# Second layer's attention as straight-line code, in batches of six key tiles instead of four

## The chip, the core and the metric

The kernel runs on one core of a Trainium2 chip. The metric is the device time of the whole program in microseconds (us), the median of several runs. TensorE (PE in the profile) multiplies matrices into PSUM, VectorE (DVE), ScalarE (ACT) and GpSimd (POOL) do elementwise work, SyncE (SP) issues most of the DMAs. Each engine works through its own list of instructions in order, and the lists are tied together by semaphores that the kernel sets by hand.

## The reference

Two layers, each with attention and a feed-forward network (FFN) that gates it, on x of shape (2, 2048, 256), 16 heads of width 16. What the change touches is the attention of the second layer:

```python
Q = _l2norm(heads(Wq)); K = _l2norm(heads(Wk)); V = heads(Wv)
cos_sim = jnp.clip(jnp.einsum('bhtd,bhsd->bhts', Q, K), -0.999, 0.999)
scores = 1.0 - jnp.arccos(cos_sim) / jnp.pi
W = jnp.power(jnp.maximum(scores, EPS), 16.0)
W = W / (jnp.sum(W, axis=-1, keepdims=True) + EPS)
out = jnp.einsum('bhts,bhsd->bhtd', W, V)          # then @ Wo.T + bo
...
x = x + s * silu(ffn(xn))                          # s: attention, xn: layernorm(x)
```

So for each of 2 x 16 pairs of batch entry and head there is a 2048 x 2048 matrix of cosines, and each element goes through a clip, an arccosine and a sixteenth power. The first layer has another weight function (inverse squared distances), which is the same before and after.

## The kernel before, in words

**Phases.** `program` runs one phase after another, each a block with a barrier at its end: constants, then for each layer `weights_phase`, `norm_phase`, `projection_phase`, `attention_phase`, `output_phase`.

**Units.** In the attention a *unit* is one key tile of 128 keys against all 2048 queries of one head and one batch entry: a [128, 2048] float32 matrix. A head has 32 units (16 for each batch entry), the layer 512. Sixteen units make one *tile of work* n (a head and a batch entry); with each n goes one 128-token tile of the FFN. There are 32 of them.

**Steps of a unit in the second layer.** TensorE writes the cosines into two PSUM halves `psS[0]`, `psS[1]` of 1024 columns (`pe_scores`, L741). VectorE clips each half into the ring in SBUF (L1049) and multiplies clipped by unclipped cosine into a ring of squares (L1058); only then may TensorE overwrite that half. ScalarE takes `Ln(1 - c^2)` (L1006) and a `Sigmoid` of it (L1011). VectorE multiplies (L1089, here called the tangents). ScalarE takes `Arctan` (L1016). The power of 16 is split by columns: ScalarE does columns 0 to 1311 by `Ln` (L1022) and `Exp` (L1028), VectorE 1312 to 1535 by an affine step (L1069) and four squarings (L1073), GpSimd 1536 to 2047 the same way (L711, L715). TensorE then multiplies with the values (`pe_values`, L764), into `psO`.

**Batches.** `Ln`/`Exp` and `Sigmoid`/`Arctan` belong to different tables of ScalarE, so the steps are done for a *batch* of 4 units at a time, and a table is loaded twice in a batch (`ACT_TABLE_LOAD` ahead of L1011 and at L1017). ScalarE's order in a batch is two `Ln`, load, four `Sigmoid`, two `Arctan`, load, two `Ln`, two `Exp`. VectorE's order is: clip and square batch j, powers of batch j-1, tangents of batch j. So in each batch the tangents wait for the sigmoids (`s_rs`), and the second `Ln` waits for the last squares (`s_q`). The ring has 8 slots of cosines and 4 of squares.

**Heads.** `pairs` writes head 0 and head 15 out and runs heads 1 to 14 in a hardware loop on SP, TensorE, ScalarE and VectorE; GpSimd's heads are written out. A loop's code for a head begins with another load of ScalarE's table (L1001).

**The FFN's part.** `pe_hidden` (L785, L791: 16 matmuls and two bias matmuls) comes on TensorE behind a batch's scores and the previous batch's weighted sums, in batches 2 and 6 of a head; `pe_ffn_sum` (L800, L803) a batch later. ScalarE's `act_relu` (L817), `act_out` (L810) and `act_ffn_out` (L823, L825) come between batches; VectorE's `dve_out` comes behind the tangents.

**Buffers.** `values` and `gated` (each [128, 32, 256]) are buffers of their own, `work` holds three times that size. The values of the second layer stay in `values`, GpSimd copies a head's part into `v_tile` (L703). The normalized head outputs go into `gated`, from which `output_phase` transposes them (L1154).

## Time and profile before

| what | us |
|---|---|
| median of 3 runs | 7601.04 (7600.39 to 7608.52) |
| the profiled execution: its own time | 7607.89 |
| the profiled execution: span of the trace | 7605.8 |
| first clip of the second layer's attention (L1049) starts at | 3018.2 |
| last clip of it starts at | 7474.3 |
| VectorE busy over the whole span | 7175.8 (94%) |
| ScalarE busy | 6931.5 (91%) |
| TensorE busy, matmuls | 4245.9 (56%) |
| GpSimd busy | 2209.8 (29%) |

The span runs from the first to the last instruction; the 2 us between it and the own time lie outside the trace. The second layer's attention takes well over half of the time. Shares of busy time are averages: which engine sets the pace of a batch has to be read from the timelines.

### The profile page before, as it was taken

The numbers are of one execution on the slowest core, as the hardware profiler recorded it, in microseconds if no ns is written. First come the engines' busy times: TensorE is split into PE (matmuls) and PEld (weight loads), VectorE is DVE, ScalarE is ACT, GpSimd is POOL, SyncE is SP. The second block draws the span as 40 slices with busy tenths as digits, with TensorE's granted clock in tenths as the row PEclk, the third lists the DMA queues.
The fourth block names the chain that finished last, engine by engine and source line by source line (L and its number), as shares of the span: only waits on it lengthen the run. The fifth ranks groups of instructions, "written<-read, shape, count | busy, mean of one in ns | idle before, by whom it ended". The sixth has DMA issues, their size and how long they took to land. (4 is left out here: it accounts for less than half of the span.)

```text
span 7605.8 us, 60658 instructions
## 1 busy us (share of the span) xinstructions
PE 4245.9 (56%) x17232; PEld 1292.8 (17%) x17232; DVE 7175.8 (94%) x6927; ACT 6931.5 (91%) x4385; POOL 2209.8 (29%) x1348
## 2 busy tenths in 40 slices
PE   6666666676766667444444454444444444544545
PEld 3221212121222233111111111111111111111112
DVE  7899999999999966999999999999999999999996
ACT  3799999999999934999999999999999999999995
POOL 0000000000000000454544445454544545454452
PEclk9888888888888878666566665656666665665667
DMA  3100000000000022000000000000000000000002
GB/s 128 43 18 11 16 12 16 12 16 12 16 12 14 10 102 102 6 11 7 6 11 6 6 11 6 6 11 6 6 11 6 10 6 6 10 6 6 10 2 69
DMA packets 113675, 148.41 MB, mean 20 GB/s; under 512 B 17038, under 2 KB 98857, under 8 KB 112634
## 3 DMA queue, kind: packets, MB, share of 16 engines
q1 hardware_dynamic: 104314, 138.54, 5.8%
q10 hardware_dynamic: 9216, 8.39, 0.3%
q14 instruction: 109, 0.89, 0.0%
q8 instruction: 36, 0.59, 0.0%
HBM read 91.55 MB, written 55.31 MB: 19 GB/s over the span
## 5 line engine op out<-in xcount | busy, mean ns | idle before, releaser
L741 PE MATMUL psS<-q_stack,k_stack 102*128 102x512 bf16 (+1 forms) x4096 | 1795.1, 534 | 2464.6 <-DVE work L1058 1617.3
L715 POOL TENSOR_TENSOR work<-work 128x1024 f32<-128x1024 f32 x1024 | 1915.4, 1907 | 10.2
L764 PE MATMUL psO<-work,v_tile 128*32 128x512 f32 x8192 | 1432.5, 822 | 732.0 <-DVE work L1073 727.5
L933 DVE SCALAR_TENSOR_TENSOR work<-work,psS 128x1024 f32<-128x1024 f32 x1024 | 1240.2, 1211 | 42.4 <-ACT work L891 41.9
L1049 DVE TENSOR_SCALAR work<-psS 128x1024 f32<-128x1024 f32 x1024 | 1206.7, 1218 | 71.0 <-issue 41.2
L1058 DVE TENSOR_TENSOR work<-psS,work 128x1024 f32<-128x1024 f32 x1024 | 1199.8, 1213 | 0.0
L1089 DVE SCALAR_TENSOR_TENSOR work<-work 128x2048 f32<-128x2048 f32 x512 | 1138.5, 2285 | 58.3 <-ACT work L1011 56.7
L891 ACT ACTIVATE work<-psS 128x1024 f32<-128x1024 f32 x1024 | 1099.6, 1074 | 70.6 <-PE psS L741 45.4
L1006 ACT ACTIVATE work<-work 128x4096 f32<-128x4096 f32 x256 | 921.2, 3612 | 126.9 <-DVE work L1058 117.1
L906 ACT ACTIVATE work<-work 128x2048 f32<-128x2048 f32 x512 | 1005.3, 1964 | 0.4 <-ACT ffn_out L823 0.4
L741 PEld LDWEIGHTS psS<-q_stack,k_stack 102*128 102x128 bf16 (+1 forms) x4096 | 257.5, 105 | 4136.7 <-DVE work L1058 2509.8
L1011 ACT ACTIVATE work<-work 128x2048 f32<-128x2048 f32 x512 | 936.0, 1899 | 1.4
L711 POOL TENSOR_SCALAR work<-work 128x1024 f32<-128x1024 f32 x256 | 267.5, 1045 | 2300.4 <-ACT work L1016 2290.2
L1016 ACT ACTIVATE work<-work 128x4096 f32<-128x4096 f32 x256 | 924.0, 3609 | 6.9
L703 POOL COPY v_tile<-values 128x256 f32<-128x256 f32 x64 | 28.4, 444 | 2996.5 <-PE psO L764 2313.0
L952 DVE TENSOR_TENSOR work<-work 128x1056 f32<-128x1056 f32 x512 | 639.2, 1249 | 0.0
L946 DVE TENSOR_SCALAR work<-work 128x2048 f32<-128x2048 f32 x512 | 623.1, 1217 | 0.0
L1022 ACT ACTIVATE work<-work 128x2624 f32<-128x2624 f32 x256 | 597.9, 2383 | 1.4
L1028 ACT ACTIVATE work<-work 128x2624 f32<-128x2624 f32 x256 | 595.7, 2374 | 0.0
L1073 DVE TENSOR_TENSOR work<-work 128x448 f32<-128x448 f32 x1024 | 571.8, 624 | 0.0
L913 ACT ACTIVATE work<-work 128x992 f32<-128x992 f32 x512 | 558.0, 1090 | 0.0
L764 PEld LDWEIGHTS psO<-work,v_tile 128*32 128x32 f32 x8192 | 253.0, 137 | 1579.4 <-issue 856.5
(126 smaller groups left out, 3444.8 us busy)
## 6 DMA issues: line engine op xcount, KB each, us to landing
qk_parts<-work SPq DMA_DIRECT2D x64, 384.0 KB, 3.2
q_stack<-qk_parts SPq DMA_DIRECT2D x384, 64.0 KB, 2.2
k_stack<-qk_parts SPq DMA_DIRECT2D x384, 64.0 KB, 2.2
ffn_in<-xT_store SPq DMA_DIRECT2D x64, 128.0 KB, 2.5
y_store<-ffn_out ACTq DMA_DIRECT2D x64, 128.0 KB, 1.7
work<-y_store SPq DMA_DIRECT2D x8, 1024.0 KB, 12.0
work<-in_x SPq DMA_DIRECT2D x1, 4096.0 KB, 14.4
xn_store<-work SPq DMA_DIRECT2D x1, 4096.0 KB, 13.0
```

Of the source, the lines that this page charges most:

```text
L715: nc.gpsimd.tensor_tensor(part, part, part, ALU.mult).then_inc(s_pp, 1)
L741: last = nc.tensor.matmul(m.psS[half][:, q * 512:(q + 1) * 512], m.k_stack[b][0:rows, kt * P:(kt + 1) * P], m.q_stack[b][0:rows, c:c + 512 ...
L764: last = nc.tensor.matmul(m.psO[b][VW * q:VW * (q + 1), :], m.v_tile[b][:, kt, :], ring[:, u % RING, q * 512:(q + 1) * 512], start=kt == 0 ...
L891: nc.scalar.activation(ring[:, u % RING, half * 1024:(half + 1) * 1024], m.psS[half][:, :], ACT.Abs_reciprocal_sqrt, bias=ZERO_SHIFT)\
L906: nc.scalar.activation(slot, slot, ACT.Abs_reciprocal_sqrt, bias=SHEP_EPS * SHEP_EPS, scale=2 * SHEP_EPS).then_inc(s_v, 1)
L933: nc.vector.scalar_tensor_tensor(part, part, 0.5 / SHEP_EPS, m.psS[half][:, :], ALU.add, ALU.mult).then_inc(s_y, 1)
L1006: nc.scalar.activation(pair, pair, ACT.Ln, bias=1.0, scale=-1.0).then_inc(s_ls, 1)
L1011: nc.scalar.activation(slot, slot, ACT.Sigmoid, scale=-0.5).then_inc(s_rs, 1)
L1016: nc.scalar.activation(pair, pair, ACT.Arctan).then_inc(s_at, 1)
L1049: nc.vector.tensor_scalar(ring[:, u % RING, half * 1024:(half + 1) * 1024], m.psS[half][:, :], COS_MAX, -COS_MAX, ALU.min, ALU.max)\
L1058: nc.vector.tensor_tensor(q_ring[:, u % BATCH, cols], m.psS[half][:, :], ring[:, u % RING, cols], ALU.mult).then_inc(s_q, 1)
L1089: nc.vector.scalar_tensor_tensor(slot, q_ring[:, u % BATCH, :], RSIN_MAX, slot, ALU.min, ALU.mult).then_inc(s_z, 1)
```

## The change

What it does:

1. `attention_phase` becomes two functions. `distance_phase` is the first layer's, as it was. `cosine_phase` is new and holds the second layer's; its code is written out for all 512 units on all engines (no hardware loop).
2. Batches have 6 units (`sizes` is 4, then 84 times 6, then 4: 86 batches instead of 128). The ring has 18 slots: 2 x 6 of cosines, 6 of squares. Batches no longer end where a tile of work ends.
3. ScalarE's instructions get larger: `Ln` and `Arctan` take half a batch (3 units, 6144 columns), `Sigmoid` two units, the power's `Ln` and `Exp` 3 x 1312 columns. The table of `Ln`/`Exp` is named again at the start of each batch. VectorE's and GpSimd's parts of the power take 3 x 224 and 3 x 512 columns. GpSimd's first step waits for the first half of the arctangents only.
4. VectorE's order in pass i is: tangents i, head output, clip and square i+1, powers i. That is the order of before, with the pass cut elsewhere.
5. TensorE: `ffn_hidden` stands in the middle of a batch's scores. Weighted sums, head output and `ffn_sum` stand behind them.
6. To make room, `values` and `gated` become parts of `work`. In the second layer the values go to DRAM (`v_store`) during the projection, and a head's part is loaded into `v_tile` by SP in pieces of 64 bytes. Each head output is stored to DRAM (`o_store`) from a small stage by a DMA that ScalarE issues, and `output_phase` loads it back, as a third load in each of its four chunks. There the transposes wait for that load.

```diff
+        self.work = sb("work", [P, 5 * NT * D])
+        self.values = self.area(3 * NT * D, NT, D)
+        self.gated = self.area(4 * NT * D, NT, D)
...
@@ projection_phase, SP
+                if L == 1:
+                    sp.wait_ge(s_vfree, 4 * i + 6)
+                    sp.dma_start(io["v_store"][:, bass.ds(4 * i, 4), :], m.values[:, bass.ds(4 * i, 4), :])\
+                        .then_inc(s_vst, 16)
...
@@ cosine_phase
+    BATCH = 6
+    LANES = 18
+    sizes = [4] + [BATCH] * ((TOTAL - 8) // BATCH) + [4]
+    starts = [sum(sizes[:j]) for j in range(len(sizes) + 1)]
+    last_batch = {n: batch_of(KT * n + KT - 1)[0] for n in range(TILES)}
+    last_batch[-1] = -2
...
+        def _(sp):
+            for n in range(TILES):
+                h, b = n // B, n % B
+                if n >= B:
+                    sp.wait_ge(s_qk, 2 * KT * (n - 1))
...
+                if n >= B:
+                    sp.wait_ge(s_pv, KT * (n - 1))
+                sp.dma_start(m.v_tile[b][:, :, 0:DH], v_view[:, b, :, h, :]).then_inc(s_vt[b], 16)
+                if n > 0:
+                    sp.wait_ge(s_h, 2 * n)
+                sp.dma_start(m.ffn_in[:, :, :], io["xT_store"][:, :, n * P:(n + 1) * P]).then_inc(s_fin, 16)
...
+        def _(pe):
+            scores(0)
+            for i in range(NB + 2):
+                ahead = range(starts[i] + 1, min(starts[i + 1] + 1, TOTAL)) if i < NB else []
+                middle = len(ahead) // 2
+                for g in ahead[:middle]:
+                    scores(g)
+                for n in range(TILES):
+                    if last_batch[n - 1] + 3 == i:
+                        ffn_hidden(n)
+                for g in ahead[middle:]:
+                    scores(g)
+                if 1 <= i <= NB:
+                    for g in range(starts[i - 1], starts[i]):
+                        weighted(g)
+                for n in range(TILES):
+                    if last_batch[n] + 2 == i:
+                        head_out(n)
+                    if last_batch[n - 1] + 3 == i:
+                        ffn_sum(n)
...
+        def _(act):
+            for i in range(NB + 2):
+                if i < NB:
+                    nc.scalar.preload_act_table_set("natural_log_exp_and_others")
+                    for c, (p, size) in enumerate(thirds(i)):
+                        act.wait_ge(s_q, 2 * (starts[i] + p + size))
+                        nc.scalar.activation(square(p, size), square(p, size), ACT.Ln, bias=1.0, scale=-1.0)\
+                            .then_inc(s_ls, 1)
+                    for p, size in couples(i):
+                        act.wait_ge(s_ls, 2 * i + (1 if p + size <= sizes[i] // 2 else 2))
+                        nc.scalar.activation(square(p, size), square(p, size), ACT.Sigmoid, scale=-0.5)\
+                            .then_inc(s_rs, 2)
+                    for p, size in thirds(i):
+                        act.wait_ge(s_z, starts[i] + p + size)
+                        nc.scalar.activation(cosine(i, p, size), cosine(i, p, size), ACT.Arctan).then_inc(s_at, 1)
+                    nc.scalar.preload_act_table_set("natural_log_exp_and_others")
...
+                for n in range(TILES):
+                    if last_batch[n - 1] + 2 == i:
+                        relu(n)
+                    if last_batch[n] + 1 == i:
+                        out_copy(n)
+                    if last_batch[n] + 2 == i:
+                        out_store(n)
+                    if last_batch[n - 1] + 3 == i:
+                        ffn_out(n)
...
+        def _(dve):
+            for g in range(starts[1]):
+                clip_and_square(g)
+            for i in range(NB + 2):
+                if i < NB:
+                    tangents(i)
+                for n in range(TILES):
+                    if last_batch[n] + 2 == i:
+                        head_out(n)
+                if i + 1 < NB:
+                    for g in range(starts[i + 1], starts[i + 2]):
+                        clip_and_square(g)
+                if i < NB:
+                    powers(i)
...
@@ output_phase
-        n_loads = 3 if L == 0 else 2
+        n_loads = 3
...
+                else:
+                    sp.dma_start(m.gated[:, t, :], io["o_store"][:, t, :]).then_inc(s_load[c], 16)
...
+                if L == 1 and n % CP == 0:
+                    pe.wait_ge(s_load[n // CP], 16 * n_loads)
```

(`thirds` gives a batch's two halves, `couples` its pairs of units.)

TensorE's order around the FFN's hidden layer, before: the end of head 15's first half. L741 are scores (16 matmuls are 4 units), L764 weighted sums, L785 and L791 the hidden layer, L800 and L803 the FFN's sum.

```order
L764 MATMUL psO<-work,v_tile 32x512 x16
L741 MATMUL psS<-q_stack,k_stack 128x512 x16
L764 MATMUL psO<-work,v_tile 32x512 x16
L785 MATMUL psM<-ffn_in,w1T 128x128 x8
L791 MATMUL psM<-ident,b_tiles 128x512
L785 MATMUL psM<-ffn_in,w1T 128x128 x8
L791 MATMUL psM<-ident,b_tiles 128x512
L741 MATMUL psS<-q_stack,k_stack 128x512 x16
L764 MATMUL psO<-work,v_tile 32x512 x16
```

The same place of the program after: L1005 are scores (24 matmuls are 6 units), L1023 weighted sums, L1044 and L1046 the hidden layer.

```order
L1031 MATMUL psM<-ident,head_outT 128x128 x4
L1005 MATMUL psS<-q_stack,k_stack 128x512 x12
L1044 MATMUL psM<-ffn_in,w1T 128x128 x8
L1046 MATMUL psM<-ident,b_tiles 128x512
L1044 MATMUL psM<-ffn_in,w1T 128x128 x8
L1046 MATMUL psM<-ident,b_tiles 128x512
L1005 MATMUL psS<-q_stack,k_stack 128x512 x12
L1023 MATMUL psO<-work,v_tile 32x512 x24
L1053 MATMUL psM<-w2T,hidden 128x256 x8
```

Before, the hidden layer stood between weighted sums and the next batch's scores. Now it stands between the third and the fourth of six units of scores.

ScalarE's order in one batch, before (L1006 `Ln`, L1011 `Sigmoid`, L1016 `Arctan`, L1022 and L1028 the power):

```order
L1006 ACTIVATE work<-work 128x4096 x2
L1011 ACT_TABLE_LOAD
L1011 ACTIVATE work<-work 128x2048 x4
L1016 ACTIVATE work<-work 128x4096 x2
L1017 ACT_TABLE_LOAD
L1022 ACTIVATE work<-work 128x2x1312 x2
L1028 ACTIVATE work<-work 128x2x1312 x2
```

and after (L1112, L1116, L1120, L1125 and L1129 in their place):

```order
L1109 ACT_TABLE_LOAD
L1112 ACTIVATE work<-work 128x6144 x2
L1116 ACT_TABLE_LOAD
L1116 ACTIVATE work<-work 128x4096 x3
L1120 ACTIVATE work<-work 128x6144 x2
L1121 ACT_TABLE_LOAD
L1125 ACTIVATE work<-work 128x3x1312 x2
L1129 ACTIVATE work<-work 128x3x1312 x2
```

Eleven instructions now serve six units where twelve served four; there are three table loads in each batch instead of two (and one more in each head).

## Rows read from the trace of the kernel before

**Rows 1.** Busy time by engine in a stretch of the cosine attention.

```profile
5000.00:7400.00 2400.00, 1134.05 (x4290) 294.20 (x4286) 2334.68 (x2105) 2328.97 (x1038) 1172.40 (x702) 0.61 0.03 7
```

**Rows 2.** Where line L1049 waited, second layer's clips, DVE; first and last start.

```profile
L1049 DVE TENSOR_SCALAR work<-psS x1024: 1210/1216/1226, 3018.2 to 7474.3; 128x1024 f32<-128x1024 f32 x171
...
  issue: 41.2, 13
```

**Rows 3.** ScalarE's timeline: start us, length us, engine, line, operation, count, idle before.

```profile
4009.70 7.12 ACT L1006 ACTIVATE work<-work 128x4096 f32<-128x4096 f32 x2 [0.62 <-ACT ffn_out L823]
...
4047.61 3.62 ACT L1006 ACTIVATE work<-work 128x4096 f32<-128x4096 f32 x1 [0.46 <-DVE work L1058]
...
4051.24 1.28 ACT L1011 ACT_TABLE_LOAD   x1
...
4052.54 7.31 ACT L1011 ACTIVATE work<-work 128x2048 f32<-128x2048 f32 x4
...
4059.75 7.27 ACT L1016 ACTIVATE work<-work 128x4096 f32<-128x4096 f32 x2
...
4068.34 4.67 ACT L1022 ACTIVATE work<-work 128x2624 f32<-128x2624 f32 x2
```

**Rows 4.** ScalarE's sigmoid of one unit, from the page's groups: mean ns.

```profile
L1011 ACT ACTIVATE work<-work 128x2048 f32<-128x2048 f32 x512 | 936.0, 1899 | 1.4
```

**Rows 5.** VectorE's timeline over the same batches.

```profile
4047.49 2.71 DVE L1069 TENSOR_SCALAR work<-work 128x448 f32<-128x448 f32 x2
...
4050.12 4.36 DVE L1073 TENSOR_TENSOR work<-work 128x448 f32<-128x448 f32 x8
...
4054.48 8.90 DVE L1089 SCALAR_TENSOR_TENSOR work<-work 128x2048 f32<-128x2048 f32 x4
...
4064.45 2.34 DVE L1049 TENSOR_SCALAR work<-psS 128x1024 f32<-128x1024 f32 x2
...
4082.82 1.96 DVE L1069 TENSOR_SCALAR work<-work 128x448 f32<-128x448 f32 x2
```

**Rows 6.** GpSimd's timeline: its chain of squarings in that batch.

```profile
4034.95 15.00 POOL L715 TENSOR_TENSOR work<-work 128x1024 f32<-128x1024 f32 x8
```

**Rows 7.** VectorE's squarings of the last batch, while GpSimd runs its own.

```profile
7499.66 17.93 DVE L1073 TENSOR_TENSOR work<-work 128x448 f32<-128x448 f32 x8
```

**Rows 8.** TensorE's timeline around one hidden layer of the feed-forward part.

```profile
4089.11 5.46 PE L764 MATMUL psO<-work,v_tile 128*32 128x512 f32 x32 [5.12 <-DVE work L1073]
...
4094.50 2.05 PE L785 MATMUL psM<-ffn_in,w1T 128*128 128x128 f32 x16
...
4099.52 1.12 PE L791 MATMUL psM<-ident,b_tiles 8*128 8x512 f32 x2
...
4102.39 0.60 PE L741 MATMUL psS<-q_stack,k_stack 96*128 96x512 bf16 x2 [1.74 <-DVE work L1058]
...
4107.00 2.16 PE L741 MATMUL psS<-q_stack,k_stack 96*128 96x512 bf16 x4 [2.45 <-DVE work L1058]
```

**Rows 9.** Windows: TensorE's granted clock (PEclk) after 4089.11, when weighted sums began.

```profile
4088.00:4092.00 4.00, 2.89 (x16) 0.79 (x20) 3.25 (x3) 4.00 (x3) 0.00 (x0) 0.50 0.00 0
...
4092.00:4096.00 4.00, 4.00 (x33) 1.94 (x26) 4.00 (x3) 4.00 (x3) 0.00 (x0) 0.90 0.00 0
```

**Rows 10.** TensorE, output phase: the same eight matmuls at either clock.

```profile
7542.95 3.78 PE L1171 MATMUL psO<-hidden,w1T 128*128 128x256 f32 x8 [7.31 <-ACT w1T L1187]
...
7548.40 1.99 PE L1171 MATMUL psO<-hidden,w1T 128*128 128x256 f32 x8
```

**Rows 11.** Output phases of first and second layer: first DMA issue, last ScalarE copy.

```profile
2713.72 0.39 SPq L1128 DMA_DIRECT2D hidden<-in_woT  x1
...
2789.55 0.60 ACT L1187 ACTIVATE w1T<-psS 128x512 f32<-128x512 f32 x1 [2.81 <-PE psO L1171]
...
7529.76 0.39 SPq L1128 DMA_DIRECT2D hidden<-in_woT  x1
...
7594.85 0.60 ACT L1187 ACTIVATE w1T<-psS 128x512 f32<-128x512 f32 x1 [2.81 <-PE psO L1171]
```

More of the change, by code:

```diff
@@ L60, in __init__ @@
         self.w2T = sb("w2T", [P, FT, D])
-        self.values = sb("values", [P, NT, D])
-        self.gated = sb("gated", [P, NT, D])
-        self.work = sb("work", [P, 3 * NT * D])
+        self.work = sb("work", [P, 5 * NT * D])
+        self.values = self.area(3 * NT * D, NT, D)
+        self.gated = self.area(4 * NT * D, NT, D)
         self.q_stack = [sb(f"q_stack{b}", [P, T], BF16) for b in range(B)]
@@ L643, in attention_phase @@
     LAG_INV, LAG_SQ = 2, 3
-    ACT_POW, DVE_POW = 1312, 1536
-    POW_STEPS = 10
-    BATCH = 4
     ACT_SQ = 992
-    rows = ROWS + NORM_ROWS if L == 0 else ROWS
-    loads = 2 * len(PRODUCTS) + (2 if L == 0 else 0)
+    rows = ROWS + NORM_ROWS
+    loads = 2 * len(PRODUCTS) + 2
     values = m.values[:, :, :].rearrange("p (b k) (h d) -> p b k h d", b=B, h=HEADS)
     gated = m.gated[:, :, :].rearrange("p (b q a) (h d) -> p b q a h d", b=B, q=QB, h=HEADS)
-    EPS_SUM = SHEP_EPS if L == 0 else SUM_EPS1
     with ExitStack() as ctx:
@@ L699, in _ @@
         def _(pool):
[L700 to L729 removed]
+            def head(h, first, last):
+                for b in range(B):
+                    if not first:
+                        pool.wait_ge(s_pv, UNITS * h + KT * b + KT - UNITS)
+                    nc.gpsimd.tensor_copy(m.v_tile[b][:, :, 0:DH], values[:, b, :, h, :]).then_inc(s_vt, 1)
+            pairs(pool, head)
         def pe_scores(pe, h, u, first, halves=(0, 1)):
@@ L736, in pe_scores @@
                 if not (first and u == 0):
-                    pe.wait_ge(s_y if L == 0 else s_q, 2 * (UNITS * h + u) + half - 1)
+                    pe.wait_ge(s_y, 2 * (UNITS * h + u) + half - 1)
                 for q in range(2):
@@ new lines, in dve_out, with head @@
+            nc.vector.tensor_tensor(out, ps[:, :, :, 0:DH], out, ALU.mult).then_inc(s_g0, 1)
+            dve.wait_ge(s_g0, n + 1)
+            nc.vector.tensor_tensor(out, out, rec16, ALU.mult).then_inc(s_g, 1)
+        OUT_COPY, OUT_T, OUT_DIV = 5, 7, 8
+        HID = (0, 1, 2, 3)
+        RELU, SQ = (2, 4), (4, 6)
+        SUM = {8: (0,), 9: (1,), 10: (2,), 11: (3,), 12: (4,), 13: (5,), 14: (6, 7)}
+        COPY = 15
+        @block.tensor
+        def _(pe):
+            def head(h, first, last):
+                for u in range(UNITS + (LAG_PV if last else 0)):
+                    b, kt = u // KT, u % KT
+                    n = 2 * h + b
+                    if u < UNITS:
+                        pe_scores(pe, h, u, first, (0,))
+                    if not (first and u < LAG_PV):
+                        pe_values(pe, h, u - LAG_PV, first)
+                    if u < UNITS:
+                        pe_scores(pe, h, u, first, (1,))
+                    if kt == 0 and not first:
+                        pe.wait_ge(s_g, n - 1)
+                    if kt == 2 and not (first and b == 0):
+                        pe.wait_ge(s_yo, n)
+                    if kt in HID and u < UNITS:
+                        pe_hidden(pe, n, (HID.index(kt),))
+                    if kt == OUT_T and u < UNITS and not (first and b == 0):
+                        pe.wait_ge(s_r, 2 * n + 1)
+                        pe_out(pe, n - 1)
+                    if kt in SUM:
+                        pe_ffn_sum(pe, n, SUM[kt])
+                if last:
+                    pe_out(pe, 2 * HEADS - 1)
+            pairs(pe, head)
```

577 lines of the change are left out of this document (284 added, 293 removed).

## The prediction, made before the run

> **What bounds the kernel now.** I read the windows first, then the clips' own line, then the engines' timelines over two batches. In a stretch of 2400 us VectorE is busy 2334.68 and ScalarE 2328.97, TensorE 1134.05, GpSimd 1172.40 [rows 1]. Two engines at 97% means that shares alone cannot say which one sets the pace. The clips give it: from 3018.2 to 7474.3 lie 127 batches, three units and one half [rows 2]. A unit of clips and squares takes (4082.82 - 4064.45) / 4 = 4.59 us [rows 5], so the last 3.25 units are 14.95, and a batch takes (4456.1 - 14.95) / 127 = 34.97 us, 8.74 per unit.
>
> Why 34.97? There are two sums. *VectorE's own work*: clips 18.37, powers 6.99 (4047.49 to 4054.48), tangents 8.90 and 0.10 behind them [rows 5]: 34.4. *The chain through both engines*: last square, 0.12 until the second `Ln` starts (4047.61), 3.62 of `Ln`, 1.30 from load to sigmoid (4051.24 to 4052.54) [rows 3], 1.90 for one sigmoid [rows 4], 0.04, tangents and gap 9.00, clips 18.37 [rows 5]: 34.4 as well. The two are level: the powers fill the 7.0 us in which ScalarE does `Ln`, load and first sigmoid. On top come a head output every fourth batch (1.07 us from the tangents' end to the next clip, 0.97 more than the gap; 0.24 per batch) and 41.2 us in 13 waits on "issue", which are the loop's restarts (0.32 per batch) [rows 2, 5]. Sum 34.96, measured 34.97.
>
> **The change part by part.**
>
> *Size of instructions.* ScalarE's cost grows by (3.62 - 1.90) / 2048 = 0.84 ns per column [rows 3, 4]. So an `Ln` of 6144 columns takes 5.34, a sigmoid of two units 3.62, a power step of 3936 columns 3.48 (2.38 for 2624). ScalarE has less to do per unit. But what VectorE must wait for is longer: the half batch of `Ln` behind the last square and the first sigmoid both grow.
>
> *The chain for six units*: 0.12 + 5.34 + 1.30 + 3.62 + 0.04 + tangents 13.35 + 0.10 + clips 27.56 = 51.43 us, 8.57 per unit against 8.60. The larger batch halves nothing: the fixed part went from 7.0 for four units to 10.4 for six. VectorE's own sum: 27.56 + 13.45 + powers. Eight squarings of 448 columns took 4.36 [rows 5], 0.545 each; 224 more columns at 1.09 ns (8.90 / 8192) make 0.79, so 6.3. The two affine steps took 2.71 because GpSimd's chain was still running (4034.95 + 15.00 = 4049.95) [rows 5, 6]; with GpSimd at 1.5 times the work it ends about as late behind the clips, so 2.7 again. Powers 9.0, VectorE 50.0. The chain is longer by 1.4, so the chain sets the pace and VectorE idles 1.4 per batch.
>
> *ScalarE's own path*, from the first sigmoid (time 0): sigmoids until 10.7, `Arctan` of the first half until 16.0; the second half needs all tangents (3.66 + 13.35 = 17.0) and ends at 22.4; load 23.7; four power steps 13.7: 37.4; the repeated load 38.7; first `Ln` 44.0. The last square comes at 44.7. So the third load fits, with 0.8 to spare. What stands between batches (the copies and their DMAs) can exceed this: `ffn_out` costs 0.62 of idle time around its DMA and its copy, about 1.0 together [rows 3], and meets a head copy of the same kind in a third of the tiles: some 8 us in all.
>
> The skill puts a table switch higher: the Trainium skill, "ScalarE: Activation LUTs", section "What ACT_TABLE_LOAD costs", gives about 1.28 us for the load and 1.38 for a drain, 2.66 in all. By that each batch's chain would be 1.4 longer (+115 us) and ScalarE's path, with three of them, 4 longer. The rows show 1.30 from load to next instruction, and the sum goes by them.
>
> *Sum over the batches.* 83 steps from six to six: 4268.7. The step from four to six has two tangents less (4.45): 47.0. The step from six to four has two clips less and a smaller `Ln` (9.18 + 1.72): 40.5. Together 4356. The first clips and `Ln` are the same four units as before (23.4). Head outputs 31 x 0.97 = 30. So 4410 from first clip to last sigmoid, against 127 x 34.97 + 23.4 = 4464.6 before: -55. About 41 of this is the loop's waits.
>
> *The hidden layer in the middle of the scores.* In the steady state TensorE scores a unit in 2.16 us and then idles 2.45 until VectorE frees the next half [rows 8]. VectorE starts on that half as soon as it is written, so 2.45 us, and about 0.5 more, is all the cover there is. The hidden layer runs from 4094.50 to 4099.52 + 1.12 = 6.14 us [rows 8]. Before, it lay beside powers and tangents: scores then still waited 1.74 for VectorE [rows 8]. Now it lies between two units that VectorE clips one after the other. And 6.14 is at the high clock, since weighted sums from 4089.11 on had raised it: the granted clock was 0.50 in the first window and 0.90 in the second, so it rose at about 4092.8, 3.7 us after they began [rows 8, 9]. Scores alone run at the low clock. Eight matmuls take 3.78 at the low and 1.99 at the high level, a factor of 1.90 [rows 10]. If the hidden layer does 4.0 us at the low level, it gets 2.1 us of work done there and takes 8.0 in all. It is late by 8.0 - 2.45 = 5.55; the next scores, now at the high clock, are 0.44 faster (0.60 against 1.04), and ends overlap a little: VectorE stalls 5.0 us. Bounds: high clock throughout 6.14 - 2.45 - 0.44 = 3.2; low clock throughout 11.7 - 2.45 = 9.2. The stall delays the clips, which are in the chain, and 32 tiles have it: +160 us (102 to 294). It is the largest term. ScalarE's relu waits for it but still reaches the `Ln` in time.
>
> The clock rule of the Trainium skill, "TensorE: Matmul & The Clock Gate", section "The HAM clock gate", is that a busy array gets 2.4 GHz and one that pauses falls to 1.2. Taken alone it does not say which level the hidden layer would meet behind scores that come with pauses; the windows show the low one, and the sum goes by them.
>
> *Values and outputs through DRAM.* The values' load is asked for when the tile before last is weighted, a whole tile (about 137 us) ahead: hidden. SP's waits for it hold back the next stacks by some units at most, of 16. The value stores in the projection are hidden but for the last (+2). At the end ScalarE's last store has to land before the barrier: +4. The output phase gets a third load in each chunk. The first layer has that form: from first DMA to last copy 75.8 us against 65.1 [rows 11]: +10.7, and 1.5 for transposes that now wait. Together +18. If this were all hidden it would be 0.
>
> **Sum.** -55 + 160 + 8 + 18 = +131 on the profiled execution's 7607.9: 7739. The median of before lies 6.9 lower, so 7732; I say 7730.
>
> **Rivals.**
>
> *A, the hidden layer is slower or faster than thought, loop as above.* Its bounds give 7730 - 58 = 7672 and 7730 + 134 = 7864. A low clock to the end needs the rise to come later than the 3.7 us seen.
>
> *B, ScalarE's path decides* (reserve 0.8 us). If the repeated load or the issue of the head's store, 2048 pieces of 64 bytes, takes 1 us more in every batch, the loop grows by 0.2 x 84 = 17; if a store holds ScalarE for 3 us, by up to 60: 7750 to 7790. Against it: the store falls into the time in which the relu waits for the hidden layer anyway.
>
> *C, GpSimd and VectorE get in each other's way.* GpSimd now starts with the first half of the arctangents, at 16.0, while VectorE's last tangent runs until 17.0. In the last batch VectorE's eight squarings took 17.93 instead of 4.36 while GpSimd ran [rows 5, 7]. If GpSimd got in ahead of that tangent, each batch would lose its affine step of about 1.6: +134, 7865. The last tangent begins 1.3 us earlier than GpSimd asks, so I expect GpSimd to be the one that waits. The Trainium skill, "SBUF — State Buffer", section "SBUF: two separate sides", calls the port pair that the two share an exclusive lock that whoever starts first holds to its end, also against a VectorE instruction with two SBUF inputs. By that rule too the tangent wins here, as long as the order stands.
>
> *D, the other side: no stall.* If scores written ahead covered the hidden layer, only -55 + 8 + 18 = -29 would be left: 7572. It decides below 0.9 us of stall per tile. Speaking for it: before, no clip waits for it. Against: there are only two halves of PSUM, and each is asked for within 4.62 us.
>
> **How the numbers follow.** Forecast (stall 4 to 6, loop by the chain) 0.50, around 7730 +- 35. A low 0.17, A high 0.13, B 0.08, C 0.05, D 0.05, a shorter chain that ends level 0.02. Range for 8 in 10: 7660 to 7830; it takes in A's low end and most of its high one, B, and leaves out C and D. A measurement of this kernel can tell about 0.2% from no change. Faster by over 0.2% comes from D and some of the last: 0.06; within 0.2% 0.04; slower 0.90.
>
> **What the profile after would show.** Clips' pitch per unit in plain batches 8.57, with ScalarE's second `Ln` waiting about 0.8 us for the square, and VectorE's tangents waiting about 1.4 for the sigmoid. In each tile one clip idle for 5 us behind TensorE's scores, in sum 160. The hidden layer's matmuls at 8 us, half of it at clock 0.5. No "issue" waits at heads. Three table loads in a batch, 1.28 each. An output phase of 76 to 78 us. Wrong would be: a clip's wait of 3 or 9 (clock), tangents that overlap GpSimd's first step (C), squares that wait for nothing (B).

## The result and the profile after

| | us |
|---|---|
| median before, 4 runs on the same chip | 7600.89 (7600.39 to 7608.52) |
| median after, 4 runs | 7718.45 (7715.76 to 7728.88) |
| ratio | 1.0155, 95% interval 1.0137 to 1.0172 |
| profiled execution after: own time, span | 7728.88, 7727.1 |

The changed kernel is slower by 118 us, 1.55%; the forecast was 7730. The profiled execution is the longest of the four.

The page of the profile after: busy times, the places where VectorE and ScalarE wait in the second layer's attention (busy total, mean ns | idle before it, what ended it).

```profile
PE 4193.2 (54%) x17232; PEld 1358.7 (18%) x17232; DVE 6988.4 (90%) x6507; ACT 6859.5 (89%) x3779; POOL 2193.3 (28%) x896
...
L1152 DVE TENSOR_SCALAR work<-psS 128x1024 f32<-128x1024 f32 x1024 | 1206.1, 1220 | 191.1 <-PE psS L1005 162.4
L1163 DVE SCALAR_TENSOR_TENSOR work<-work 128x2048 f32<-128x2048 f32 x512 | 1135.2, 2287 | 245.9 <-ACT work L1116 245.9
...
L1112 ACT ACTIVATE work<-work 128x6144 f32<-128x6144 f32 (+1 forms) x172 | 909.2, 5286 | 136.5 <-DVE work L1157 134.8
```

The same two groups of VectorE in the kernel before:

```profile
L1049 DVE TENSOR_SCALAR work<-psS 128x1024 f32<-128x1024 f32 x1024 | 1206.7, 1218 | 71.0 <-issue 41.2
L1089 DVE SCALAR_TENSOR_TENSOR work<-work 128x2048 f32<-128x2048 f32 x512 | 1138.5, 2285 | 58.3 <-ACT work L1011 56.7
```

VectorE went from 94% to 90% and ScalarE from 91% to 89%: both wait more than before. VectorE computes the same and waits in two places. The clips (L1152) wait 162.4 for TensorE's cosines, 15.7 of it ahead of the very first clip, and the tangents (L1163) wait 245.9 for ScalarE's sigmoids, where they waited 56.7 before. ScalarE in its turn waits for VectorE ahead of the second `Ln` of most batches and (99.9 in all) ahead of the second `Arctan`. Each waits for the other in turn: that is a chain through both.

VectorE's timeline after, one batch with a hidden layer in it and the next one (start, duration, operation, count, [idle before it]).

```profile
4289.14 2.36 DVE L1152 TENSOR_SCALAR work<-psS 128x1024 f32<-128x1024 f32 x2
4291.41 2.35 DVE L1157 TENSOR_TENSOR work<-psS,work 128x1024 f32<-128x1024 f32 x2
4293.83 2.36 DVE L1152 TENSOR_SCALAR work<-psS 128x1024 f32<-128x1024 f32 x2
...
4303.04 2.36 DVE L1152 TENSOR_SCALAR work<-psS 128x1024 f32<-128x1024 f32 x2 [4.59 <-PE psS L1005]
...
4322.67 13.30 DVE L1163 SCALAR_TENSOR_TENSOR work<-work 128x2048 f32<-128x2048 f32 x6 [3.13 <-ACT work L1116]
4336.01 2.36 DVE L1152 TENSOR_SCALAR work<-psS 128x1024 f32<-128x1024 f32 x2
...
4363.98 1.68 DVE L1171 TENSOR_SCALAR work<-work 128x672 f32<-128x672 f32 x2
4365.58 6.22 DVE L1174 TENSOR_TENSOR work<-work 128x672 f32<-128x672 f32 x8
4374.39 2.29 DVE L1163 SCALAR_TENSOR_TENSOR work<-work 128x2048 f32<-128x2048 f32 x1 [2.59 <-ACT work L1116]
```

The plain batch runs from tangents at 4322.67 to tangents at 4374.39: 51.72 us for six units. Against [rows 5], a unit of clips is 4.69 instead of 4.59 (4293.83 - 4289.14; the squares end at 4293.76, so 0.07 lie ahead of the next clip). In the batch ahead of it, the fifth of the six units of clips was late by 4.59.

TensorE's timeline after, at that stall.

```profile
4294.64 3.62 PE L1044 MATMUL psM<-ffn_in,w1T 128*128 128x128 f32 x16
4298.19 1.17 PE L1046 MATMUL psM<-ident,b_tiles 8*128 8x512 f32 x2
4299.29 2.05 PE L1044 MATMUL psM<-ffn_in,w1T 128*128 128x128 f32 x16
4301.27 1.12 PE L1046 MATMUL psM<-ident,b_tiles 8*128 8x512 f32 x2
4302.33 1.04 PE L1005 MATMUL psS<-q_stack,k_stack 96*128 96x512 bf16 x4
```

The windows over the same stretch (busy time of each engine, then granted clock).

```profile
4296.00:4298.00 2.00, 2.00 (x11) 1.96 (x10) 2.00 (x3) 2.00 (x1) 2.00 (x2) 0.50 0.00 0
4298.00:4300.00 2.00, 2.00 (x10) 1.05 (x9) 0.45 (x1) 1.65 (x2) 2.00 (x2) 0.92 0.00 0
```

The first 16 matmuls of the hidden layer take 3.62 at the low clock (0.50, 1.2 GHz), the second 16 take 2.05 at the high one. In all the hidden layer takes 7.75 (over the 32 tiles 7.70 in the mean), and in [rows 8] it took 6.14. VectorE has nothing to clip meanwhile: busy 0.45 in the last window, with the clock at 0.92.

ScalarE's timeline after: the batch that starts at the stall, and the start of the next.

```profile
4303.05 1.28 ACT L1109 ACT_TABLE_LOAD   x1
4304.34 5.33 ACT L1112 ACTIVATE work<-work 128x6144 f32<-128x6144 f32 x1
4312.38 5.33 ACT L1112 ACTIVATE work<-work 128x6144 f32<-128x6144 f32 x1 [2.72 <-DVE work L1157]
4317.73 1.28 ACT L1116 ACT_TABLE_LOAD   x1
4319.02 10.64 ACT L1116 ACTIVATE work<-work 128x4096 f32<-128x4096 f32 x3
...
4336.01 5.33 ACT L1120 ACTIVATE work<-work 128x6144 f32<-128x6144 f32 x1 [1.14 <-DVE work L1163]
...
4364.09 5.33 ACT L1112 ACTIVATE work<-work 128x6144 f32<-128x6144 f32 x1 [0.27 <-DVE work L1157]
4369.44 1.28 ACT L1116 ACT_TABLE_LOAD   x1
4370.73 7.13 ACT L1116 ACTIVATE work<-work 128x4096 f32<-128x4096 f32 x2
```

With the two timelines the 51.72 is one sum along the chain: tangents 13.34 (4322.67 to 4336.01), clips and squares 28.08 (to 4364.09), second `Ln` 5.35 (to 4369.44), load 1.29 (to 4370.73), the first sigmoid of two units 3.66 (to 4374.39).

**Where the 121 us of the profiled execution lie** (span 7605.8 to 7727.1). Before the first clip: -4.8 (3013.43 against 3018.2); this holds 8.6 by which the first layer's output phase, whose code is the same, took less (67.3 against 75.8). From first clip to the last batch's first sigmoid (7589.69): 4576.3 against 4464.5, so +111.8. Behind it: +14.3, nearly all in the output phase, which took 78.3 instead of 65.1 [rows 11].

### The profile page after: what moved, and what is told of

Its sections match the earlier page's. It is cut to its first block and busy times, and to the rows that moved or that the text cites. A ratio compares the mean times of both kernels' runs of the same rounds, so it can differ in the third digit from the quotient of the medians.

```text
span 7727.1 us, 55371 instructions
## 1 busy us (share of the span) xinstructions
PE 4193.2 (54%) x17232; PEld 1358.7 (18%) x17232; DVE 6988.4 (90%) x6507; ACT 6859.5 (89%) x3779; POOL 2193.3 (28%) x896
## 5 line engine op out<-in xcount | busy, mean ns | idle before, releaser
L1005 PE MATMUL psS<-q_stack,k_stack 96*128 96x512 bf16 x2048 | 1025.4, 606 | 2050.3 <-DVE work L1157 1983.8
L1214 POOL TENSOR_TENSOR work<-work 128x1536 f32<-128x1536 f32 (+1 forms) x688 | 1853.9, 2729 | 6.9
L1152 DVE TENSOR_SCALAR work<-psS 128x1024 f32<-128x1024 f32 x1024 | 1206.1, 1220 | 191.1 <-PE psS L1005 162.4
L1163 DVE SCALAR_TENSOR_TENSOR work<-work 128x2048 f32<-128x2048 f32 x512 | 1135.2, 2287 | 245.9 <-ACT work L1116 245.9
L889 DVE SCALAR_TENSOR_TENSOR work<-work,psS 128x1024 f32<-128x1024 f32 x1024 | 1249.6, 1220 | 44.1 <-ACT work L847 43.8
L712 PE MATMUL psS<-q_stack,k_stack 102*128 102x512 bf16 x2048 | 764.5, 462 | 789.3 <-DVE work L889 770.1
L1211 POOL TENSOR_SCALAR work<-work 128x1536 f32<-128x1536 f32 (+1 forms) x172 | 326.5, 1898 | 2869.9 <-ACT work L1120 2869.9
L1112 ACT ACTIVATE work<-work 128x6144 f32<-128x6144 f32 (+1 forms) x172 | 909.2, 5286 | 136.5 <-DVE work L1157 134.8
L862 ACT ACTIVATE work<-work 128x2048 f32<-128x2048 f32 x512 | 1004.9, 1963 | 0.4 <-ACT ffn_out L783 0.4
L1120 ACT ACTIVATE work<-work 128x6144 f32<-128x6144 f32 (+1 forms) x172 | 907.6, 5277 | 99.9 <-DVE work L1163 99.9
L1023 PE MATMUL psO<-work,v_tile 128*32 128x512 f32 x4096 | 652.4, 803 | 516.6 <-issue 413.3
L1116 ACT ACTIVATE work<-work 128x4096 f32<-128x4096 f32 x256 | 907.9, 3610 | 1.0
L730 PE MATMUL psO<-work,v_tile 128*32 128x512 f32 x4096 | 694.3, 757 | 4.7 <-DVE work L908 4.5
L1005 PEld LDWEIGHTS psS<-q_stack,k_stack 96*128 96x128 bf16 x2048 | 135.3, 109 | 2900.1 <-DVE work L1157 2771.0
L1125 ACT ACTIVATE work<-work 128x3936 f32<-128x3936 f32 (+1 forms) x172 | 585.6, 3452 | 1.0
L1129 ACT ACTIVATE work<-work 128x3936 f32<-128x3936 f32 (+1 forms) x172 | 584.2, 3444 | 0.0
```

Source lines behind the costliest of these rows:

```text
L712: last = nc.tensor.matmul(m.psS[half][:, q * 512:(q + 1) * 512], m.k_stack[b][0:rows, kt * P:(kt + 1) * P], m.q_stack[b][0:rows, c:c + 512 ...
L862: nc.scalar.activation(slot, slot, ACT.Abs_reciprocal_sqrt, bias=SHEP_EPS * SHEP_EPS, scale=2 * SHEP_EPS).then_inc(s_v, 1)
L889: nc.vector.scalar_tensor_tensor(part, part, 0.5 / SHEP_EPS, m.psS[half][:, :], ALU.add, ALU.mult).then_inc(s_y, 1)
L1005: last = nc.tensor.matmul(m.psS[half][:, q * 512:(q + 1) * 512], m.k_stack[b][0:ROWS, kt * P:(kt + 1) * P], m.q_stack[b][0:ROWS, c:c + 512 ...
L1112: nc.scalar.activation(square(p, size), square(p, size), ACT.Ln, bias=1.0, scale=-1.0)\
L1116: nc.scalar.activation(square(p, size), square(p, size), ACT.Sigmoid, scale=-0.5)\
```

## The experiments

All are timed beside the kernel before, whose medians were 7601.27, 7600.36 and 7601.03 in the three sets. My theory had two causes of equal rank, both in VectorE's waits: the hidden layer in the midst of the scores stalls the clips; and the pieces handed over between VectorE and ScalarE grew with the batch, so that the fixed part of each batch grew with it. The rivals are ScalarE's third table load, the waits of straight-line code, and the batch size itself. Each kernel was profiled once, so waits and durations come from one execution and the times from the medians.

| kernel | median | range | ratio to before, 95% |
|---|---|---|---|
| e1_hidden_behind | 7586.6 | 7584.14 to 7596.61 | 0.9985, 0.9976 to 0.9995 |
| e2_hidden_quarters | 7644.6 | 7640.13 to 7646.86 | 1.0059, 1.0042 to 1.0075 |
| e3_no_reload | 7724.92 | 7716.01 to 7729.96 | 1.0161, 1.0144 to 1.0177 |
| e4_one_pv_wait | 7724.41 | 7718.43 to 7728.53 | 1.0166, 1.0149 to 1.0183 |
| e5_six_coarse | 7558.64 | 7553.62 to 7563.73 | 0.9942, 0.9925 to 0.9959 |
| e6_six_fine | 7367.65 | 7364.06 to 7370.81 | 0.9692, 0.9676 to 0.9709 |
| e7_four | 7549.1 | 7547.31 to 7551.64 | 0.9931, 0.9915 to 0.9948 |
| e8_no_third_load | 7588.59 | 7579.12 to 7590.62 | 0.9981, 0.9970 to 0.9991 |
| e9_after_fine | 7566.07 | 7561.41 to 7573.4 | 0.9953, 0.9936 to 0.9970 |
| e10_before_hidden_mid | 7773.58 | 7772.45 to 7783.88 | 1.0228, 1.0211 to 1.0245 |

**e1_hidden_behind: the hidden layer behind the weighted sums.** Relu, `ffn_sum` and `ffn_out` come a batch later, and TensorE's part of the head output also waits for the relu.

```diff
-                for n in range(TILES):
-                    if last_batch[n - 1] + 3 == i:
-                        ffn_hidden(n)
...
+                        ffn_hidden(n)
+                    if last_batch[n - 1] + 4 == i:
                         ffn_sum(n)
```

> The changed kernel with one thing moved: the FFN's hidden layer stands behind the weighted sums instead of between the third and fourth unit's scores (relu, FFN sum and its copy come one batch later). My theory (the hidden layer is late for the next scores by 4.6 us in each of 32 tiles, and VectorE's clips are in the chain that sets the pace): the 143 us of clips waiting for TensorE go to nearly nothing; ScalarE gets a little later between batches (relu and copies now fall where it has 0.8 us to spare), giving back 10 to 20 us. Time 7718 - 125 = 7593, between 7575 and 7610. Rival (the stall lies in time in which VectorE would wait for ScalarE anyway, so that its removal only moves the wait to the tangents): the wait of the tangents grows from 246 to about 390 us and the time stays at 7700 or above.

The groups of the clips and of the tangents in e1:

```profile
L1152 DVE TENSOR_SCALAR work<-psS 128x1024 f32<-128x1024 f32 x1024 | 1205.4, 1219 | 49.8 <-PE psS L1005 17.5
L1163 DVE SCALAR_TENSOR_TENSOR work<-work 128x2048 f32<-128x2048 f32 x512 | 1135.0, 2285 | 246.5 <-ACT work L1116 246.5
```

Of the 17.5, 15.8 is the very first clip. The stall is gone, and 132 us with it; the tangents' wait has not moved. So the stall was on the path nearly one to one (147 us in the clips), and it is more than the whole loss against before.

**e10_before_hidden_mid: the same, done to the kernel before.** The hidden layer goes between the second and the third unit's scores of a batch; nothing else is changed.

```diff
+                            if j % 4 == 3 and u == BATCH * j + 3:
...
+                                pe_hidden(pe, n)
...
-                        if j % 4 == 2:
...
-                            pe_hidden(pe, n)
```

> The kernel before with one part of the change: the hidden layer stands between the second and third unit's scores of a batch (batches of four, loops, all else as before). My theory: 32 stalls of 4.6 us (hidden layer 7.7 us at a clock that starts low, less 2.5 idle, less a little) in the chain: 7601 + 147 = 7748, between 7720 and 7780. Rival (in batches of four the stall falls into a wait for ScalarE): below 7680.

The clips' group in e10:

```profile
L1049 DVE TENSOR_SCALAR work<-psS 128x1024 f32<-128x1024 f32 x1024 | 1206.1, 1219 | 243.5 <-PE psS L741 187.9 <-issue 40.9 <-DVE work L1089 3.8
```

It cost 172.6 us, and the clips wait 173.6 for TensorE beside their first wait of 14.3. The place alone makes a kernel slower, with batches of four as with batches of six. The stall is 5.4 per tile where after has 4.6, because the hidden layer takes 8.48 in the mean (6.99 to 11.34, six tiles at 11.3) at this place; I had expected that it behaves as in after, and the time lies in the upper part of my range.

**e2_hidden_quarters: the hidden layer in four parts,** one behind each of the first four units' scores.

```diff
+                for at in range(max(len(ahead), 4)):
+                    if at < len(ahead):
+                        scores(ahead[at])
+                    if at < 4:
+                        for n in here:
+                            ffn_hidden(n, at)
```

> The changed kernel with the hidden layer cut into four quarters, one behind each of the first four units' scores of the batch. The same work in the same stretch of the batch; only the longest piece between two scores shrinks from 6 to 8 us to 1.5 (high clock) or 2.9 (low clock), against 2.5 us of idle time and some 0.4 more. My theory (a piece costs only what exceeds the cover): clips wait at most 0.3 us per quarter, in sum below 40 us instead of 143, time 7718 - 110 = 7608, between 7590 and 7635. Rival (the place itself costs, by PSUM or by the relu of ScalarE that waits for it): waits in sum as before, time above 7690.

Missed by 37 us, 10 above the range. The clips' stall is nearly gone, as expected (44.1 with the first wait, so 28). But the relu now gets its input late in the batch. The groups of tangents, `Ln` and relu in e2:

```profile
L1164 DVE SCALAR_TENSOR_TENSOR work<-work 128x2048 f32<-128x2048 f32 x512 | 1134.9, 2285 | 290.3 <-ACT work L1117 290.3
...
L1113 ACT ACTIVATE work<-work 128x6144 f32<-128x6144 f32 (+1 forms) x172 | 905.4, 5282 | 52.6 <-DVE work L1158 50.9
...
L1097 ACT ACTIVATE hidden<-psM 128x512 f32<-128x512 f32 x64 | 37.4, 585 | 101.8 <-PE psM L1048 101.8
```

The relu waits 101.8 (none in e1), the second `Ln` then hardly waits for squares any more (50.9, 93.3 in e1), and the tangents wait 44 more (290.3 against 246.5). The place has a second price, through ScalarE. In the kernel after the relu waits 87.0 too, but there the squares are late as well, and the `Ln` still waits for them.

**e3_no_reload: the third table load taken out.**

```diff
-                    nc.scalar.preload_act_table_set("natural_log_exp_and_others")
+                    if i == 0:
+                        nc.scalar.preload_act_table_set("natural_log_exp_and_others")
```

> The changed kernel without the repeated table load at the start of each batch (85 loads of 1.28 us less). My theory (ScalarE reaches the second Ln early, the last square decides): the loads were nearly hidden, time 7718 - 0 to 8 us. Rival (ScalarE's path is as long as the chain): up to 85 x 1.3 = 110 us less, 7610.

No change: 7724.92, 6 us above after, with ranges that overlap. `Ln` waits for the squares 250.7 instead of 134.8, so 116 us return as a wait; 85 loads at 1.28 are 109 of them. Rival B's load costs nothing in this kernel.

**e4_one_pv_wait: VectorE asks once per batch, not once per unit, whether the weighted sums have freed the slots.**

```diff
-                if j >= 2:
-                    dve.wait_ge(s_pv, starts[j - 2] + min(p + 1, sizes[j - 2]))
+                if j >= 2 and p == 0:
+                    dve.wait_ge(s_pv, starts[j - 1])
```

> The changed kernel with one wait of VectorE for the weighted sums at a batch's first clip instead of one at each unit's. In the changed kernel a unit of clips and squares takes 4.69 us, before the change 4.60; the 0.07 to 0.09 us stand ahead of the first clip. If the second semaphore that this clip waits for is the reason, the unit falls to 4.62 and the time by about 30 us to 7690. If it is TensorE's scores at the low clock that end just then (they take 1.04 us from the first square's end), nothing changes.

Missed: no gain (7724.41 against 7718.45). The unit did become shorter. VectorE's timeline in e4:

```profile
4336.09 2.36 DVE L1152 TENSOR_SCALAR work<-psS 128x1024 f32<-128x1024 f32 x2
...
4340.71 2.36 DVE L1152 TENSOR_SCALAR work<-psS 128x1024 f32<-128x1024 f32 x2
```

4.61 per unit instead of 4.69, and the tangents wait 228.0 instead of 245.9. Against it stands TensorE: in the profiled execution the hidden layer takes 8.47 in the mean (6.70 to 11.34, nine tiles at 11.3), and the clips wait 189.4 instead of 162.4. What is idle ahead of clips beside that wait fell from 28.7 to 2.6, so the clips' idle time is the same in the two (192.0 and 191.1): the 26 us that the edit gave went into the longer stall. One of the longest, in TensorE's timeline of e4:

```profile
3430.21 3.62 PE L1044 MATMUL psM<-ffn_in,w1T 128*128 128x128 f32 x16
...
3435.76 3.78 PE L1044 MATMUL psM<-ffn_in,w1T 128*128 128x128 f32 x16
3439.48 2.07 PE L1046 MATMUL psM<-ident,b_tiles 8*128 8x512 f32 x2
```

And the windows of e4 over its two halves (clock in the third column from the end):

```profile
3430.00:3436.00 6.00, 6.00 (x20) 4.18 (x20) 3.94 (x4) 4.89 (x3) 6.00 (x3) 0.50 0.05 5
3436.00:3441.50 5.50, 5.50 (x19) 3.77 (x20) 0.00 (x0) 0.53 (x1) 5.50 (x3) 0.50 0.00 0
```

The second 16 matmuls took 3.78, not 2.05: all of it ran at the low clock. Why the clock rose within the hidden layer in every tile of the kernel after and not in these nine is open, and so is whether the edit has to do with it.

**e5_six_coarse: e1, e3 and e4 together.** The pieces are those of the change.

> Batches of six as in the change, with the hidden layer behind the weighted sums, no repeated table load and one wait for the weighted sums per batch. It is the base of the next two. In the run that made only the last edit the unit of clips fell from 4.69 to 4.61 us, but the hidden layer in the middle of the scores grew from 7.7 to 8.5 us on the mean and took it back. With the hidden layer out of the way my theory lets the gain through: 0.075 x 512 = 38 us, partly behind ScalarE's path, and some 10 for the loads: 7587 - 40 = 7547, between 7535 and 7565. Rival (the unit's 0.07 us never was in the chain): 7575 to 7587.

7558.64, within the range. The change without its stall is e1, 14 us faster than before; with the edits of e3 and e4 as well it is 42 us faster. The 28 us between e1 and e5 look like those of e4's edit: what is idle ahead of clips beside the wait for TensorE is 32.3 in e1 and 3.2 in e5. Tangents still wait 225.0.

**e6_six_fine: e5 with smaller pieces at the two hand-overs.** `Ln` over four units and then two, `Sigmoid` over 1, 1, 2 and 2.

```diff
+    def logs(j):
+        first = sizes[j] - 2
+        return [(0, first), (first, 2)]
+
-        return [(p, 2) for p in range(0, sizes[j], 2)]
+        return [(0, 1), (1, 1)] + [(p, 2) for p in range(2, sizes[j], 2)]
```

> The base with six units, and ScalarE's pieces at the two places where VectorE waits made small again: Ln over 4 and then 2 units instead of 3 and 3, Sigmoid over 1, 1, 2, 2 units instead of three times 2. The fixed part of the chain (last square to first tangent) falls from 10.4 to 6.95 us. My theory (this part, and not the number of units, is what a batch of six lost): VectorE's powers (7.9 us) then fill it, the tangents' wait of 246 us in 85 batches goes, and a batch takes 27.7 + 7.9 + 13.45 = 49.1 us of VectorE's own work against 51.3: 7547 - 84 x 1.9 = 7390, between 7370 and 7440. Rival (ScalarE's own work sets the pace, 49.2 with what stands between batches, plus waits for half batches of tangents): 7440 to 7500.

7367.65: 191 us less than e5, 3.1% less than before, the best of all, and 2 us below the range. `Ln` and `Sigmoid` were cut finer together, so which of the two gives how much is not known. ScalarE's timeline in e6, at the hand-over:

```profile
4363.44 3.62 ACT L1117 ACTIVATE work<-work 128x4096 f32<-128x4096 f32 x1 [1.40 <-DVE work L1162]
4367.08 1.28 ACT L1121 ACT_TABLE_LOAD   x1
4368.37 7.22 ACT L1121 ACTIVATE work<-work 128x2048 f32<-128x2048 f32 x3
```

VectorE's timeline in e6, from tangents to tangents:

```profile
4321.15 4.48 DVE L1168 SCALAR_TENSOR_TENSOR work<-work 128x2048 f32<-128x2048 f32 x2
4325.96 8.90 DVE L1168 SCALAR_TENSOR_TENSOR work<-work 128x2048 f32<-128x2048 f32 x4 [0.32 <-ACT work L1121]
...
4363.33 1.21 DVE L1176 TENSOR_SCALAR work<-work 128x672 f32<-128x672 f32 x2
...
4370.60 2.28 DVE L1168 SCALAR_TENSOR_TENSOR work<-work 128x2048 f32<-128x2048 f32 x1
```

From last square to first tangent there are now 3.6 of `Ln`, 1.3 of load and 1.9 of sigmoid, 6.8 in all instead of 10.3. VectorE's powers take 7.3 (4363.33 to 4370.60), so they fill it, and the tangents follow with no wait. A window of e6 as long as the one of [rows 1] (PE, PEld, DVE, ACT, POOL busy, clock):

```profile
4000.00:6400.00 2400.00, 1158.64 (x4520) 315.61 (x4524) 2378.79 (x2000) 2356.81 (x755) 1199.67 (x487) 0.60 0.05 10
```

In e6 VectorE is busy 99% (over the same 2400 us it is 2330.77 before, 97%, and 2321.16 in e7): its own work sets the pace now, and no longer the chain. ScalarE, at 98%, is close behind.

**e7_four: batches of four again** in this code, with the pieces of the kernel before (`Ln` over two units, single sigmoids). It has the same steps as e5, only batch and pieces are smaller. The groups of clips and tangents in e7:

```profile
L1153 DVE TENSOR_SCALAR work<-psS 128x1024 f32<-128x1024 f32 x1024 | 1207.6, 1219 | 19.0 <-PE psS L1005 15.6
L1164 DVE SCALAR_TENSOR_TENSOR work<-work 128x2048 f32<-128x2048 f32 x512 | 1138.8, 2286 | 143.3 <-ACT work L1117 143.3
```

> The base with batches of four, Ln and Arctan over 2 units, Sigmoid over single units, as before the change, but written out, through DRAM and with the other edits of the base. It tells what six units in coarse pieces are worth against four in the old pieces. By the chain four units take 34.4 us, 8.60 per unit, and six in coarse pieces 51.3, 8.55 per unit. With head outputs the same in both: 7547 + 25 = 7572, between 7555 and 7595. Rival (larger instructions and fewer table loads pay by themselves, ScalarE's busy time falls by 0.2 us per unit): four would be 80 to 120 us slower than six coarse, 7630 to 7670.

7549.1, 6 us below the range. Four units (7549) and six in coarse pieces (7559) are within 10 us: a batch half as large again, cut into pieces that grow with it, is worth nothing. Six units paid when the last piece of `Ln` and the first of `Sigmoid` stayed as small as with four: 7368. Four units in still finer pieces were not tried.

e7 also shows about what straight-line code does. It has the batches and pieces of the kernel before, with the way through DRAM, and is 51 us faster: the clips' idle time fell from 71.0 to 19.0, and the 41.2 of "issue", the loop's restarts, are gone. It gains no more because the tangents wait longer (143.3 against 56.7), as VectorE's affine steps in front of them got shorter (210.2 in all against 299.1).

**e9_after_fine: the kernel after with the fine pieces alone** (the diff of e6 applied to it, nothing else).

> The changed kernel as it is (hidden layer amid the scores, repeated load, a wait per unit), with only ScalarE's pieces made small: Ln over 4 and 2 units, Sigmoid over 1, 1, 2, 2. It undoes the second of my two causes alone. My theory (the two add up: a stall of 4.6 us in each of 32 tiles, and 10.4 us between last square and first tangent, of which VectorE fills 7.4 to 7.9): 7718 falls by 140 to 190 us, as from 7559 to 7368 without the stalls, less what ScalarE's repeated load now costs, since its own work comes to 50.5 us a batch: 7565, between 7530 and 7600; clips still wait 140 to 160 us for TensorE. Rival (stall and coarse pieces hide each other): above 7640.

7566.07, as expected: 152 us less than after. The tangents' wait falls from 245.9 to 83.6, and the clips' wait stays at 162.7. With e1 this shows the two causes apart: 132 and 152. In e6 both are gone, and it is 351 us below after; the 67 us beyond their sum come with the edits of e3 and e4. 28 of them are the difference of e1 and e5. For the rest, the tangents wait 83.6 in e9 and 39.6 in e6, which fits a repeated load that costs something once the pieces are fine; that was not tested by itself.

**e8_no_third_load: e1 without the load of the head outputs from DRAM.** It leaves that data out: the transposes of the second layer's output phase take what lies in the buffer.

> The kernel with the hidden layer behind the weighted sums, without the load of the head outputs in the second layer's output phase (it leaves that data out: the transposes read what lies in the buffer). The output phase from first DMA to last copy took 65.1 us before the change and 78.3 after. If the third load is the reason: 78.3 - 12 = 66 us, and the time 7587 - 12 = 7575. Rival (the transposes' wait for the loads is the reason, not the load's bytes): 75 us or more.

Missed: its median is that of e1 (7588.59 against 7586.6). From the phase's first DMA to the last copy the profiled executions have 65.3 against 68.7. The load costs 3.4 us, less than the runs scatter. The transposes still wait for the loads here, and 65.3 against 65.1 before gives that wait no price. The 78.3 of after, from which I had reckoned, was not the load's.

## Why the prediction was right, point by point

**The chain.** Forecast 51.43 per batch, measured 51.72. The forecast had the right sum: clips and squares with the gap behind them were 0.40 longer (28.08 against 27.68, a unit 4.69), the tangents 0.11 shorter (13.34 against 13.45), and from `Ln` to the first sigmoid's end it was 10.30 in both. First clip to last batch's first sigmoid: the forecast's steps add up to 4356 + 23.4 + 30 + 160 + 8 = 4577; measured 4576.3. That they agree so closely is in part two misses that cancel: the loop gained 35 (111.8 - 147) instead of 47 (55 less 8 for copies), and the stall was 147 instead of 160.

**The stall.** Forecast 5.0 in each of 32 tiles from a hidden layer of 8.0, half of it at the low clock. Measured 4.6 from 7.70, 3.6 of it at the low clock. e1 and e10 show that it sits on the path one to one, from both sides. It was the largest term and decided the sign. Its size is in part luck: I had the clock's rise from one place of the trace. In after all 32 tiles took 6.94 to 7.96, but at the same place in e4 nine and in e9 four of 32 stayed at the low clock throughout (11.3), which was the upper end of rival A.

**VectorE's powers** were put at 9.0 and VectorE's idle time ahead of the tangents at 1.4. They took 7.8 (the affine pair 1.15 to 1.68, not 2.7), and the idle time is 2.9 per batch (245.9 in 85). This didn't touch the time, since the chain passes by the powers, but it hid from me how much there was to win, and e6 won much of it.

**The third load of ScalarE** was taken to fit with 0.8 to spare. It did (e3). The Trainium skill, "ScalarE: Activation LUTs", section "What ACT_TABLE_LOAD costs", would have 2.66 for a switch; here load and sigmoid lie 1.29 apart after as well (4369.44, 4370.73).

**GpSimd and the tangents (rival C).** Its first affine step started while the last tangent ran and took 2.35 us where the next took 1.47, and six tangents took 13.30, as forecast (13.35). So it was GpSimd that waited. GpSimd's timeline after:

```profile
4334.96 2.35 POOL L1211 TENSOR_SCALAR work<-work 128x1536 f32<-128x1536 f32 x1 [27.45 <-ACT work L1120]
4341.41 1.47 POOL L1211 TENSOR_SCALAR work<-work 128x1536 f32<-128x1536 f32 x1 [4.11 <-ACT work L1120]
```

The step that starts at 4334.96 is the one beside the last tangent, which ends at 4335.97; the step ends 1.34 later. By the rule of the Trainium skill that the prediction named under rival C ("SBUF — State Buffer", section "SBUF: two separate sides") the last tangent, which had started first, keeps the port; the trace agrees.

**Rival B's stores.** The `o_store` issue took 0.40 on ScalarE's queue and landed 3.0 later; it held nothing back.

**Rival D**, no stall, was put at 7572. The kernels in which the stall was taken out are e1 with 7587 and e5, with two edits more, with 7559.

**The output phase** is the step that was wrong: its size came out (78.3, forecast 76 to 78), but by luck, since its cause was another. I had taken the 10.7 us between the two layers' phases of [rows 11] for the third load. After, the first layer's phase, with its three loads as before, took 67.3 (2715.60 to 2782.85), the second's 78.3. e8 gives the load at 3.4. The rest is TensorE's clock, as the windows over the start of the second layer's phase show. In the kernel after:

```profile
7660.00:7670.00 10.00, 10.00 (x21) 5.66 (x20) 1.64 (x3) 0.60 (x1) 0.00 (x0) 0.50 1.06 374
7670.00:7680.00 10.00, 10.00 (x27) 6.07 (x27) 2.77 (x4) 3.00 (x3) 0.00 (x0) 0.62 0.44 152
```

In e1:

```profile
7525.00:7535.00 10.00, 10.00 (x43) 6.67 (x42) 3.93 (x7) 3.53 (x4) 0.00 (x0) 1.00 1.09 374
```

The first row of after and the row of e1 are both the second stretch of 10 us of the phase's matmuls. In after the engine did 21 matmuls at clock 0.50, in e1 43 at 1.00. The slow stretch that I had priced as a load was TensorE's clock in the first phase of before (0.50 until about 38 us after the first DMA, in the same phase of e10 until about 21), and it came again in the second phase of after. The twelve profiles hold 24 such phases, two each, measured from first DMA to last copy. Four are long: before's first (75.8), after's second (78.3), e3's second (81.5), e5's first (79.2). The other twenty took between 64.3 and 69.1, among them the second phase of e1, e4 and e6 with code like after's. The first phase of e10, whose code up to there is that of before, took 68.4. So the long form seems to come with an execution, not with the kernel. It may also be why after's profiled execution is 10 us above its median; that was not tested. A third load is worth +3.4. With this in place of 10.7 and 1.5, my term of +18 would have been about +9; measured were -4.8 ahead of the first clip and +14.3 at the end, 9.5 in all, with a slow phase on either side of the comparison.

## What to carry to other kernels

Where two engines pass a batch back and forth, the time between batches is the last piece of one plus the first piece of the other, and it grows with the batch if the pieces are cut as fractions of it: make the middle pieces large and keep the last one in and the first one out small (191 us here), and then see that the work held back for that gap fills it. Put a foreign block of matmuls behind a stage whose consumer has other work, not between two products that it takes one after the other, and cost it at the clock that its neighbours leave (7.7 us here instead of 6.1). A difference between two phases of one profile is a cost of their code only when a second execution shows it again.

## What the runs showed of the hardware that was not expected

- TensorE's granted clock stayed at 0.50 through stretches without a pause: 7660 to 7670 of after (busy 10.00 of 10), and 11.34 us of hidden layer in e4, e9 and e10, while in after the hidden layer never took over 7.96. The Trainium skill, "TensorE: Matmul & The Clock Gate", section "The HAM clock gate", has a busy array at 2.4 GHz; for these stretches the rows say otherwise. What sets them apart is open.
- A second semaphore wait ahead of a clip costs 0.07 us in the straight-line code (4.69 against 4.61 per unit, e4). The kernel before has two such waits too, at 4.59. Why it costs nothing there was not tried.
- Storing a head output as 2048 pieces of 64 bytes holds the issuing queue for only 0.40 us and lands after 3.0.
